# Top-2 gate scores in two halves instead of one piece, in an attention and mixture-of-experts kernel on eight cores

## What is computed

```python
x = L0_attn_x                                   # 32 x 2048 x 1024, f32
x = x + attention(layernorm(x), W_qkv, W_proj, b_proj)   # linear attention, 16 heads
x = x + ffn(layernorm(x), gate_w, gate_b, expert_w, expert_b)

def _L0_ffn_ref(x, gate_w, gate_b, expert_w, expert_b):  # E = 8 experts, K = 2
    logits = jnp.einsum('bsd,ed->bse', x, gate_w) + gate_b
    topv, topi = jax.lax.top_k(logits, K)
    keep = jax.nn.one_hot(topi, E, dtype=jnp.float32).sum(axis=-2)
    logits = jnp.where(keep > 0, logits, -jnp.inf)
    gate_score = jax.nn.softmax(logits, axis=-1)
    expert_out = jnp.einsum('bsd,edo->bseo', x, expert_w) + expert_b
    return jnp.einsum('bseo,bse->bso', expert_out, gate_score)
```

## Time and profile before

| what | us |
|---|---|
| median of the timed runs | 4044.56 |
| the timed runs (2) | 4032.12 and 4057.01 |
| the profiled execution | 3947.61 |
| its span, slowest core (core 1) | 3946.0 |
| spans of the other cores | 3901.4 to 3937.2 |
| PE busy | 3141.2 (80%) |
| DVE busy | 1095.7 (28%) |
| ACT busy | 606.4 (15%) |

### The profile page before, as it was taken

How to read it: one execution, slowest core, us unless ns; L and a number is a source line. 1 busy time by engine, 2 the same in 40 slices (tenths; PEclk the granted TensorE clock), 3 DMA queues, 4 the chain that set the end, 5 groups by cost and what they waited for, 6 DMA issues and landing times.

```text
span 3946.0 us, 44114 instructions; the slowest of 8 cores (3901.4 to 3946.0 us)
## 1 busy us (share of the span) xinstructions
PE 3141.2 (80%) x18304; PEld 1514.8 (38%) x18304; DVE 1095.7 (28%) x1380; ACT 606.4 (15%) x985; POOL 138.6 (4%) x171
## 2 busy tenths in 40 slices
PE   1987569999088767999909876899990987589998
PEld 0443324444044333444404433444440443344443
DVE  3223512222221343222222135322213123532221
ACT  2343100000133320000013332000002433100000
POOL 0000000000000000000000000000000000000000
PEclk9988679999598878999959887899995988689999
DMA  9031591111500042111150003211115000321111
GB/s 227 30 65 43 91 235 22 17 20 19 176 1 6 38 137 82 22 17 22 17 176 1 17 38 139 75 17 19 19 20 172 1 22 38 133 75 17 22 16 22
DMA packets 71077, 229.58 MB, mean 58 GB/s; under 512 B 9250, under 2 KB 21538, under 8 KB 65634
## 3 DMA queue, kind: packets, MB, share of 16 engines
q0 software_dynamic: 38768, 75.71, 12.0%
q1 hardware_dynamic: 32114, 151.04, 10.8%
HBM read 159.76 MB, written 92.27 MB: 64 GB/s over the span
## 4 chain that ended last, share of the span: by engine, by line
PE 77%; DVE 7%; DMA 6%; ACT 3%; issue 3%; SPq 3%; another core or an unknown queue 1%; DVEq 0%; POOL 0%; ACTq 0%; POOLq 0%
PE pb L127 74%; DMA xres<-x 3%; PE pbt L127 3%; SPq L127 3%; DVE q_s L127 2%; DVE attB L127 2%; ACT q_s L127 2%; DMA we<-scr_we 1%; DVE lnx L127 1%; DMA sel<-sel 1%; ACT attA L127 1%; DVE r_all L127 1%; DVE st L127 0%; DVEq L127 0%
## 5 line engine op out<-in xcount | busy, mean ns | idle before, releaser
L127 PE MATMUL pb<-we,lhsT_lo 128*128 128x512 bf16 x4096 | 903.7, 382 | 9.7 <-DMA we<-scr_we 8.8
L127 PE MATMUL pb<-we,lhsT_hi 128*128 128x512 bf16 x4096 | 894.5, 379 | 0.0
L127 PEld LDWEIGHTS pb<-we,lhsT_lo 128*128 128x128 bf16 x4096 | 397.6, 98 | 513.4 <-issue 50.1
L127 PEld LDWEIGHTS pb<-we,lhsT_hi 128*128 128x128 bf16 x4096 | 400.9, 98 | 483.2
L127 PE MATMUL pb<-wkv_s,lnx 128*128 128x512 bf16 x2048 | 455.2, 385 | 41.2 <-DMA gb_s<-gb 25.7
L127 ACT ACTIVATE q_s<-xres 128x1024 bf16<-128x1024 f32 x128 | 135.2, 1056 | 1928.7 <-DMA xres<-x 1651.1
L127 PE MATMUL pbt<-ident,q_s 128*128 128x128 bf16 x1024 | 102.7, 273 | 398.3 <-DVE q_s L127 386.5
L127 DVE TENSOR_TENSOR lhsT_hi<-lnx,z 128x4096 bf16<-128x4096 bf16 x64 | 146.7, 2292 | 691.3 <-PE pb L127 691.3
L127 DVE TENSOR_TENSOR lhsT_lo<-lnx,z 128x4096 bf16<-128x4096 bf16 x64 | 146.7, 2292 | 629.0 <-PE pb L127 628.6
L127 PEld LDWEIGHTS pb<-wkv_s,lnx 128*128 128x128 bf16 x2048 | 201.8, 99 | 289.8 <-issue 58.1
L127 PE MATMUL pb<-wp_s,attA 128*128 128x512 bf16 x1024 | 273.6, 415 | 25.1 <-ACT attA L127 25.1
(11 more groups left out here) (69 smaller groups left out, 1305.1 us busy)
## 6 DMA issues: line engine op xcount, KB each, us to landing
we<-scr_we SPq DMA_DIRECT2D x24, 2048.0 KB, 17.0
out<-xres SPq DMA_DIRECT2D x64, 512.0 KB, 2.6
out<-otmp POOLq DMA_DIRECT2D x128, 256.0 KB, 5.1
xres<-x POOLq DMA_DIRECT2D x8, 2048.0 KB, 27.1
xres<-x SPq DMA_DIRECT2D x8, 2048.0 KB, 33.2
we<-ew POOLq DMA_DIRECT2D x8, 2048.0 KB, 24.5
scr_we<-we SPq DMA_DIRECT2D x8, 2048.0 KB, 26.3
wkv_s<-scr_wkv SPq DMA_DIRECT2D x12, 1024.0 KB, 27.6
```

Of the source, the lines that this page charges most:

```text
L127: last = getattr(eng, name)(*a, **kw)
```

## The change

The top-2 chain is written as `emit_top2_half(h)`, for tiles 0 to 7 and for tiles 8 to 15. The first half is emitted in the loop over the tiles, right behind the logits of tile 7 (the end of chunk 1), and the second right behind those of tile 15. Each half has the same 12 DVE and 2 ACT instructions, on 128x64 and 128x8 elements, and 2 of the 4 rounds of transposes and copies. The region `scoresT` becomes `scoresT0` and `scoresT1`.

```diff
+        t2b = 4 * max(1, (NT // 2) // 4)
+        self._t2split = t2b
+
+        def emit_top2_half(h):
+            lo = 0 if h == 0 else t2b
+            hi = t2b if h == 0 else NT
+            HT = hi - lo
+            sl = slice(lo * E, hi * E)
+            ss = slice(lo, hi)
+
+            def f_t2(eng, h=h):
+                k.wait_w(eng, "vector", "gate")
+                k.inc(eng.tensor_reduce(
+                    k.m1.ap()[:, ss], v3(k.lgraw.ap()[:, sl]),
+                    axis=AX.X, op=ALU.max), "s_v")
...
+            for t4 in range(lo, hi, 4):
+                def f_st(eng, t4=t4):
+                    k.wait_w(eng, "tensor", "gate")
+                    k.wait_w(eng, "tensor", "ident")
+                    k.wait_rw(eng, "tensor", "bank6")
...
+                self.on("tensor", f_st)
+
+                def f_ste(eng, t4=t4, h=h):
+                    nj = min(4, NT - t4)
+                    k.wait_w(eng, "vector", "bank6")
+                    k.wait_rw(eng, "vector", f"scoresT{h}")
...
+                self.on("vector", f_ste)
@@ -1096,12 +1211,17 @@
             self.on("vector", f_ge)
+            if t == t2b - 1:
+                emit_top2_half(0)
+            elif t == NT - 1:
+                emit_top2_half(1)
@@ -1124,113 +1244,9 @@
-        def f_t2(eng):
...
-            self.on("vector", f_ste)
@@ -1296,7 +1312,7 @@
             def f_em(eng, t=t, banks=banks):
-                k.wait_w(eng, "tensor", "scoresT")
+                k.wait_w(eng, "tensor", f"scoresT{0 if t < self._t2split else 1}")
```

More of the change, by code:

```diff
@@ L639, in emit_batch @@
             self.merge_region("attA", dst)
-            self.merge_region("scoresT", dst)
+            self.merge_region("scoresT0", dst)
+            self.merge_region("scoresT1", dst)
             self.merge_region("eb_s", dst)
@@ L1102, in emit_batch @@
             self.emit_expert_load(e, b)
-        self.merge_region("attA", "scoresT")
+        self.merge_region("attA", "scoresT0")
+        self.merge_region("attA", "scoresT1")
         self.merge_region("attA", "eb_s")
@@ L1125, in emit_batch @@
         k.note_w("sel8", "s_we", wetot)
-        def v3(ap):
-            return ap.rearrange("p (t e) -> p t e", e=E)
-        def f_t2(eng):
[L1131 to L1225, removed]
-            self.on("vector", f_ste)
@@ L1228, in emit_batch @@
-        if cut == "gate":
-            return
         def emit_z8(t):
             def f_z8(eng, t=t):
-                k.wait_w(eng, "tensor", "scoresT")
+                k.wait_w(eng, "tensor", f"scoresT{0 if t < self._t2split else 1}")
                 k.wait_w(eng, "tensor", "sel8")
@@ L1246, in f_z8 @@
                         k.note_w(f"bank{bank}", "s_pe", i)
-                k.note_r("scoresT", "s_pe", k.cnt("s_pe"))
+                k.note_r(f"scoresT{0 if t < self._t2split else 1}", "s_pe", k.cnt("s_pe"))
             self.on("tensor", f_z8)
@@ L1334, in f_em @@
                                 k.note_r(f"we{ee}", "s_pe", i)
-                            k.note_r("scoresT", "s_pe", i)
+                            k.note_r(f"scoresT{0 if t < self._t2split else 1}", "s_pe", i)
                             k.note_r("eb_s", "s_pe", i)
@@ L1391, in emit_batch @@
                     self.merge_region(f"we{e}", nm)
-        self.merge_region("scoresT", "attA")
+        self.merge_region("scoresT0", "attA")
+        self.merge_region("scoresT1", "attA")
         self.merge_region("eb_s", "attA")
```

80 lines of the change are left out of this document (added).

## The result

| | us |
|---|---|
| before, median of 42 timed runs | 3967.63 (3927.28 to 4124.67) |
| changed, median of 43 timed runs | 3970.76 (3960.70 to 4168.71) |
| ratio changed / before | 1.0069, 95% interval 1.0053 to 1.0085 |
| changed, profiled execution | 3967.99, span 3966.4 |

The changed kernel is 0.69% slower, clear of noise and within the 2% of "same". On 3967.6 us the ratio is +27 us, where +29.4 was forecast. The time itself, 3970.8 us, lies outside the stated range of 4040 to 4105. The medians are closer together than the ratio says because the ratio leaves out executions in which the cores of one or both dies (cores 0 to 3 and 4 to 7) were granted a lower TensorE clock.

The account below looks back on a forecast made before the run. Bound: the expert-load transfer released by each gate stage's last transposes. Four sequences × 7.4 us, less nothing for the second half, gave about +29.4 us: 4044.56 + 29.4 = 4074 us, range 4040 to 4105.

Parts of the forecast that it names:

- What bounds the kernel: Gate stage: FFN start is set by chunk 3's last transposes plus a transfer of about 18 us (40 in the first).
- two signs that the prediction named: Second sequence: `lhsT_lo` ready about 7 us before the FFN; FFN start less than 5 us late would mean wrong.
- The granted clock of the FFN: TensorE in the FFN: granted clock 1.00, nothing gained by longer rest; leaving 1.00 would mean the prediction is wrong.
- The price of the first half: Between chunks 1 and 2: PE waits for the early half chain; chunk 2's 32 transposes start 7.4 us later (6.8 to 7.96).
- The gain of the second half: End of gate stage: compute path 3.2 us nearer to the last transposes, but gain 0 on core 1.
- hidden price: FFN start: chunk 3's shift does not reach it; +17 us (4061) if only the compute path counts, 4045 without price; 8%.
- Nothing absorbs the shift, four sequences on the slowest core: Chunk 2 to FFN: chunk 3, last transposes, loads and landing all move; four sequences × 7.4 us, about +29.4 us.
- The rule that breaking up instructions may let work finish sooner: Skill's rule for unsaturated DVE and ACT: the halved chain would free the FFN earlier, the case of "Faster".
- Faster: PE before chunk 2's transposes: first half runs free in gaps, second half's 3.2 us count; −13 us, 4032; 2%.
- Dearer: Transfer of experts 5 to 7: later start meets other traffic, landings at their slowest, slow clock; +40 us, 4085; 6%.
- the last addition: Whole kernel: +29.4 us added to the timed median 4044.56 instead of the profiled 3947.6, giving 4074 us, 0.7% more.

Follow-up runs that it names:

- e7_same: The kernel before, unchanged, run and profiled once more against itself; ratio 1.0007 (0.9973 to 1.0041).
- the exchange: Loads of experts 6 and 7 issued ahead of expert 5: ratio to before 0.9934 in the kernel before, 0.9954 in the changed one.
- the banks alone: Kernel before with four gate-logit banks and score transposes in two rounds of eight, expert load order unchanged; two timed executions, no ratio, stages −7.6 us.

## Why the prediction was right and wrong

*What bounds the kernel: right for the changed kernel, nearly so for the one before.* In the sequences 2 to 4 of the changed kernel PE's wait before the FFN is put down to `we<-scr_we` in 23 of the 24 instances (8 cores, 3 sequences). In the other, on core 0, it is put down to DVE's cast into `z`, with `lhsT_lo` ready 3.8 us before. In the kernel before it was the compute path that ended last on four of the eight cores in the third sequence (FFN 22.0 us after the last transposes); the prediction had seen this on core 3 and gone by core 1. Taking two of the three loads out of it moved the FFN forward by 22.8 us in the first sequence.

The transfer is not of one length, though, and two signs that the prediction named fail for this reason in the second sequence. From the last transposes to the FFN it took 24.0 us before and 21.8 us in the changed kernel (medians; 22.2 and 23.1 in the third sequence). So `lhsT_lo` was ready 4.3 us before the FFN, not 7, and on the cores 1, 2, 3 and 7 the FFN came only 3.4 to 4.9 us later against the start of the stage, where less than 5 was to count as wrong. The profile of the same kernel before in `e7_same` has 22.9 us in this place, and there the difference is 6.3 us. The granted clock of the FFN stayed at 1.00, as forecast: a window of 300 us in each of the four FFNs shows it on all eight cores of both kernels.

*The price of the first half: right, 7.4 forecast, 7.5 measured* as 7.62 − 0.11 us on core 4; over the cores the last transposes come 7.3 to 7.6 us later. The halved DVE steps took what the slope between the 128x128 and 128x16 rows said. Groups by shape in the second half chain of core 4, against the earlier trace rows:

```profile
L127 ACT ACTIVATE gt<-gt 128x64 f32<-128x64 f32 x1 | 0.3, 256 | 1.0 <-DVE gt L127 1.0
...
L127 DVE TENSOR_TENSOR scores<-gt,rden 128x64 f32<-128x64 f32 x1 | 0.2, 226 | 0.1
...
L127 DVE TENSOR_TENSOR ed<-m,m 128x8 f32<-128x8 f32 x1 | 0.2, 168 | 0.1
```

226 ns against a forecast of 293 − 67 = 226, and 256 against 309 − 54 = 255.

*The gain of the second half: mis-sized, without effect.* The compute path behind the last transposes shrank by 21.75 − 17.5 = 4.2 us, not 3.2. The missing microsecond is in the rows at 1516.61 and 1517.12 above. `emit_z8(0)` waits for `scoresT0` alone, which was ready long ago, so PE runs the `sel` matmuls right behind the transposes, without waiting for the last copy. I had counted the instructions and the rounds and passed over the renamed region in the diff, which removes a wait. On the rival "hidden price" this matters: I had put 7.4 − 3.2 = 4.2 us on each sequence where the compute path counts, and the kernels with exchanged loads show 3.1 to 3.5.

*Nothing absorbs the shift, four sequences on the slowest core: right in the sum.* The last transposes came later by 30.0 us in all, the four stages grew by 7.3, 5.3, 8.2 and 6.9 us, 27.7 in all (28.9 against the kernel before in `e7_same`). The difference is that of the landings against the last transposes: −0.3, −2.2, +0.9 and −0.7 us. Between the two profiles of the kernel before they differ by up to 1.1 us as well. That forecast and measurement agree to 2 us is in part luck.

*The rule that breaking up instructions may let work finish sooner* (the Trainium skill, Perfetto Trace Analysis, Optimizing Scalar/DVE Operations) brought nothing here. The split finished the second part sooner and cost more at its first. With the transfer shortened, where the rule has its best case, it still lost 15.2 us in the sum of the stages.

*The rivals.* "Faster" needed PE to reach the transposes less than 3.2 us late; it was 7.5. "Dearer" needed landings at their slowest in all sequences. Core 4, the slowest in this profile, had 20.38 and 20.86 us in two, and its own four stages grew by 38.5 us, close to the rival's 40. But on the other seven cores they grew by 24 to 34 us, and the ratio is over many executions.

*The step that failed is the last addition, "I add the same: 4044.56 + 29.4 = 4074".* The difference was right to 2 us and the base was wrong by 77: the runs show 3967.63 us for the kernel before, in single executions from 3927 to 4125. Two timed runs were shown, 4032.12 and 4057.01, and the profiled execution at 3947.61. I wrote that the profile does not say where the 97 us lie, then took the two runs as the kernel's time with 12 us of scatter. Of the 42 runs of the kernel before that there are now, those two among them, 20 are at 3948 us or less and only 9 at 4032 or more. The two runs agreed with each other and were both from the upper tail. The profiled execution, 3947.61 us, lies at the upper edge of those 20; 3977 us, the figure the text also gives, is 6 us from the median measured, with some luck, as the two medians measured lie only 3 us apart. The range should have reached down to it. The spread between the profiled and the timed executions, 97 us, was the only measure of the base's uncertainty at hand, and the 25 us between two runs was not one.

## What to carry to other kernels

Before a chain is split so that a part runs early, look at what waits in the queue of each engine at the new place, and at what those instructions release. Here a wait of 7.5 us ahead of transposes moved a transfer that ends last. Find what ends last by its releaser, and shorten what stands between that releaser and the end: the order of three loads was worth 25 us of gate stage, while 4 us off a chain beside them were worth nothing. Once the DMA engines are busy all the time, as in the first sequence with the exchange, an earlier release buys nothing either. And anchor a time in us at several runs or at none. Where the profiled execution and the timed ones differ by more than the effect, the range has to hold both.

## What the runs showed of the hardware

The scatter goes with the granted clock. In some executions the granted clock of some cores is 0.81 in the dense stretches of the projection and attention stages, where it is 0.94 to 1.00 in others. Windows of the kernel before with the exchange, core 0 and then core 4 of the same execution (the number ahead of the last two is the granted clock):

```profile
160.00:200.00 40.00, 36.77 (x279) 17.96 (x281) 5.08 (x8) 13.27 (x22) 0.00 (x0) 0.81 0.00 1
200.00:240.00 40.00, 38.54 (x263) 17.66 (x265) 2.99 (x9) 15.72 (x26) 1.82 (x2) 0.81 0.16 26
...
160.00:200.00 40.00, 37.10 (x299) 18.45 (x298) 6.45 (x9) 15.73 (x26) 0.00 (x0) 0.94 0.00 1
200.00:240.00 40.00, 38.91 (x297) 18.94 (x296) 2.99 (x9) 20.21 (x35) 1.83 (x2) 1.00 0.29 42
```

Core 0 got 263 matmuls done in the second window where core 4 did 297, and reached `negm` of the first sequence at 461.4 us, core 4 at 445.8. Those 16 us are over half of what the change costs in all. But the lead is not kept: by `negm` of the fourth sequence it is 3.0 us, and the two spans are 3895.3 and 3891.7 us. So this row shows how far a stage can shift, not what the clock cost the execution. A lower clock that lasts does cost: in one execution of the kernel with the banks alone, four cores had a mean granted clock of 0.81 and spans of 4210 to 4240 us, while the other four had 0.88 to 0.89 and 3908 to 3922.

The Trainium skill (TensorE: Matmul & The Clock Gate, Part 1, on the clock gate) names, for the default power profile, a peak-current limit that takes a whole die to 13/16 of the clock, which is 0.81, when three of its cores run dense matmuls, and holds it while the load lasts. The level agrees with these rows. The rest does not hold for every execution here: all eight cores run the FFN at the same time, and from 550 to 850 us (and in the same part of the other three FFNs) all eight had a granted clock of 1.00 in the profiles of both kernels. That a lower clock explains the 97 us of the two timed runs is not shown, since they have no trace.
